# Graph attention block: one 512 KB transposing transfer for both heads of a unit, in place of two of 256 KB

## The chip, the cores and the metric

The kernel runs on one core of a Trainium2 chip. The metric is the device time of one execution in microseconds. Beside it there is one profiled execution, whose span runs from its first to its last instruction.

## The reference, cut to what matters

For each of 16 batches of 1024 rows and 512 columns, the block computes attention with 8 heads of width 64 under a 0/1 matrix, a projection, and two layer norms.

```
qkv = (x @ w_qkv).reshape(b, n, 3, H, hd).transpose(2, 0, 3, 1, 4)
q, k, v = (qkv[0], qkv[1], qkv[2])
attn = jnp.einsum('bhnd,bhmd->bhnm', q, k) * scale
attn = jnp.where(attn_mask[None, None] == 0, -jnp.inf, attn)
attn = jax.nn.softmax(attn, axis=-1)
o = jnp.einsum('bhnm,bhmd->bhnd', attn, v).transpose(0, 2, 1, 3).reshape(b, n, d)
o = o @ w_proj + b_proj
ln = (o - mu) * jax.lax.rsqrt(var + LN_EPS) * ln_gamma + ln_beta
x = _layernorm(x + (o + ln), axis=-1)
```

Products are made from float16 numbers in two parts, a high half (the value rounded to float16) and a low half (what is left of it), so that each product takes three matmuls.

## The kernel before, in words

The work is cut into 64 **groups** (16 batches times 4 pairs of heads) and each group into 8 **units** of 128 query rows. A unit has two **heads**, `ab` 0 and 1, which are numbered on through the group: unit u has heads 2u and 2u+1, so that a group has heads 0 to 15. The program is one loop over groups with the engines' orders written out by hand in 32 slots per group, 4 to a unit; `ORDER` and `ITEMS` spread the other matmuls of a group (projections Q, K, V, the output projection P, transposes O and XT) over the slots.

A head of a unit goes through these steps. TensorE computes scores for both heads (`unit_scores`), VectorE adds the mask and takes the row's minimum into `p32` (L616), ScalarE takes the exponential (`exponential`, L479), then one unit later ScalarE writes the high half `p_hi` (`high_part`, L492) and GpSimd the low half `p_lo` (`low_part`, L722). SyncE sends both halves through a transposing transfer into `pt` (`turn`, L279). TensorE multiplies `pt` by the values three units after the scores (`times_v`, L408 to L410; `PV_LAG` is 3).

The buffers that tie these steps: `p32`, `p_hi` and `p_lo` have `RING` = 4 places, two units. So ScalarE may write the high half of a head only when the transposes of the head four before it have landed (semaphores `turned`, 16 steps for each half). `pt` has `TURNED` = 8 places, four units. SyncE does nothing in the loop but the transposes, in the order high 0, high 1, low 0, low 1 of a unit; each issue is preceded by a wait on `hi_done` or `lo_done` (how many halves ScalarE or GpSimd has finished), and for the high half also on `pv_done`, which tells that the place in `pt` is free.

GpSimd does, between low halves, steps of the layer norm: a power (L735, L738), the bias (L732) and the output (L741). One of the outputs stands between the low halves of heads 12 and 13, the other ahead of head 4. Loads and stores of `x_res` and `x_in` are issued by ScalarE. In every fourth group the next batch's input is transposed on TensorE (XT), in units 3 and 4.

Of the kernel before, what the change touches and what calls it, by code (L numbers as in the profile page):

```python
# [17 lines left out]
UNITS = T  # L18
QUARTERS = 4
SLOTS = UNITS * QUARTERS  # L20
RING = 4
TURNED = 8
# [48 lines left out]
def known(g):  # L71
    return isinstance(g, int)


def active(g, kind):

    if not known(g):
        return True
    low, high = {"A": (0, GROUPS), "Q1": (0, GROUPS), "V0": (0, GROUPS), "V1": (0, GROUPS), "O0": (0, GROUPS),
                 "O1": (1, GROUPS + 1), "Q0": (-1, GROUPS - 1), "K0": (-1, GROUPS - 1), "K1": (-1, GROUPS - 1),  # L80
                 "P0": (PAIRS, GROUPS + PAIRS), "P1": (PAIRS, GROUPS + PAIRS)}[kind]
    return low <= g < high
# [12 lines left out]
def side_done(g, kind):  # L95

    return side_before(g) + (side_index(g, kind) + 1)
# [18 lines left out]
def unit_before(g, u, back):  # L116
    return (g, u - back) if u >= back else (g - 1, u - back + UNITS)
# [7 lines left out]
def wait(eng, sem, value):  # L125

    if known(value) and value <= 0:
        return
    eng.wait_ge(sem, value)


def wait_alone(eng, sem, value):

    if known(value) and value <= 0:
        return
    eng.wait_ge(sem, value)
    eng.nop(nofuse=True)


def attention_block(nc, x, adj, w_qkv, w_proj, b_proj, gamma, beta, out):  # L140
# [3 lines left out]
    with ExitStack() as ctx:  # L144
        def sb(name, shape, dt):
            return ctx.enter_context(nc.sbuf_tensor(name, shape, dt))

        def sem(name):
            return ctx.enter_context(nc.semaphore(name))

        def sems(name, n):
            return [sem(f"{name}{i}") for i in range(n)]

        HI, LO = 0, 1
# [14 lines left out]
        p_hi = sb("p_hi", [P, RING, N], F16)  # L169
        p_lo = sb("p_lo", [P, RING, N], F16)  # L170
        pt = sb("pt", [P, 2, TURNED, T, P], F16)
# [38 lines left out]
        x_in_loaded, x_res_loaded, stored = sems("x_in_loaded", T // 2), sems("x_res_loaded", 2), sems("stored", 2)  # L210
        s_ready, min_done, exp_done = sem("s_ready"), sem("min_done"), sem("exp_done")
        hi_done, lo_done = sem("hi_done"), sem("lo_done")
        turned = sems("turned", TURNED)
        pv_done, recip_done, o_done = sem("pv_done"), sem("recip_done"), sem("o_done")
        side_ready, side_act, side_dve = sem("side_ready"), sem("side_act"), sem("side_dve")
        xt_ready, xt_act, xt_dve = sem("xt_ready"), sem("xt_act"), sem("xt_dve")
# [6 lines left out]
        def bodies(eng, body):  # L223

            for g in range(FIRST_GROUP, LOOP[0]):
                body(g)
            with eng.Fori(LOOP[0], LOOP[1]) as g:
                body(g)
            for g in range(LOOP[1], LAST_GROUP + 1):
                body(g)  # L230
# [9 lines left out]
        def heads(g, u, ab):  # L240

            return g * (2 * UNITS) + (2 * u + ab)

        def turned_before(g, u, ab):

            return g * (32 * 2 * UNITS // TURNED) + 32 * ((2 * u + ab) // TURNED)

        def normalised(g, u):

            return g * (UNITS // NORM_UNITS) + u // NORM_UNITS  # L250
# [5 lines left out]
        @block.sync  # L256
        def _(sp):
            for t in range(T // 2):
                sp.dma_start(x_in[:, t, :, :], x_pairs[t, :, :, :]).then_inc(x_in_loaded[t], 16)
                sp.dma_start(w_in[:, t, :], w_qkv[t * P:(t + 1) * P, :]).then_inc(w_loaded, 16)  # L260
            for t in range(ADJ_SLOTS):
                sp.dma_start(adj_in[:, t, :], adj[t * P:(t + 1) * P, :]).then_inc(adj_loaded[t], 16)
            for t in range(ADJ_SLOTS, T):
                sp.wait_ge(mask_ready, t - ADJ_SLOTS + 1)
                sp.dma_start(adj_in[:, t % ADJ_SLOTS, :], adj[t * P:(t + 1) * P, :]).then_inc(adj_loaded[t % ADJ_SLOTS], 16)
            for kc in range(KC):
                sp.dma_start(wp_in[:, kc, :], w_proj[kc * P:(kc + 1) * P, :]).then_inc(wp_loaded, 16)
            for dst, src in ((gamma_b, gamma), (beta_b, beta)):
                sp.dma_start(dst[:, :], src.rearrange("(o n) -> o n", o=1).broadcast_to([P, D])).then_inc(const_loaded, 16)
            for row in (0, BIAS_LO):  # L270
                sp.dma_start(x_res[row:row + 1, 0, :], b_proj.rearrange("(o n) -> o n", o=1)).then_inc(const_loaded, 16)
            sp.wait_ge(mask_ready, T)

            def turn(g, u, ab, half, source, done):
                head = 2 * u + ab
                wait_alone(sp, done, heads(g, u, ab) + 1)
                if half == HI:
                    wait_alone(sp, pv_done, heads(g, u, ab) - (TURNED - 1))
                sp.dma_start_transpose(pt[:, half, head % TURNED, :, :], source[:, head % RING, :]  # L279
                                       ).then_inc(turned[head % TURNED], 16)  # L280

            def body(g):
                for u in range(UNITS):
                    ug, uk = unit_before(g, u, 1)
                    running = active(ug, "A")
                    if running:
                        turn(ug, uk, 0, HI, p_hi, hi_done)
                        turn(ug, uk, 1, HI, p_hi, hi_done)
                    if running:
                        turn(ug, uk, 0, LO, p_lo, lo_done)  # L290
                        turn(ug, uk, 1, LO, p_lo, lo_done)

            bodies(sp, body)
            for i in range(2):
                sp.wait_ge(stored[i], 16 * B * T // 2)

        @block.tensor
        def _(pe):
# [92 lines left out]
            def times_v(g, u, ab):  # L391

                ug, uk = unit_before(g, u, PV_LAG)
                if not active(ug, "A"):
                    return
                slot = (2 * uk + ab) % TURNED
                wait_alone(pe, turned[slot], turned_before(ug, uk, ab) + 32)
                if ab == 0:
                    if uk % NORM_UNITS == 0:
                        wait_alone(pe, o_done, normalised(ug, uk))  # L400
                    if uk == 0:
                        wait_alone(pe, side_dve, side_done(g, "V1"))
                at = (uk % NORM_UNITS * 2 + ab) * HD
                o = pv_bank[:, at:at + HD]
                for kt in range(T):
                    hi, lo = pt[:, HI, slot, kt, :], pt[:, LO, slot, kt, :]
                    v_hi, v_lo = v_both[:, kt, ab, 0:HD], v_both[:, kt, ab, HD:2 * HD]
                    nc.tensor.matmul(o, hi, v_hi, start=(kt == 0 and at == 0), stop=False, skip_group_check=True)  # L408
                    nc.tensor.matmul(o, hi, v_lo, start=False, stop=False, skip_group_check=True)  # L409
                    mm = nc.tensor.matmul(o, lo, v_hi, start=False, stop=(kt == T - 1), skip_group_check=True)  # L410
                mm.then_inc(pv_done, 1)

            def body(g):
                for u in range(UNITS):
                    if active(g, "A"):
                        unit_scores(g, u)
                    for j in range(QUARTERS):
                        if j % 2:
                            times_v(g, u, j // 2)
                        for kind, i in ITEMS[u * QUARTERS + j]:  # L420
                            side_matmul(g, kind, i)
# [4 lines left out]
        def _(act):  # L426
# [55 lines left out]
            def high_part(g, u, ab):  # L482

                ug, uk = unit_before(g, u, 1)
                if not active(ug, "A"):
                    return
                head = 2 * uk + ab
                before = unit_before(ug, uk, RING // 2)
                if not known(before[0]) or before[0] >= 0:
                    wait(act, turned[(head - RING) % TURNED], turned_before(before[0], before[1], ab) + 32)  # L490
                act.wait_ge(exp_done, heads(ug, uk, ab) + 1)
                nc.scalar.activation(p_hi[:, head % RING, :], p32[:, head % RING, :], ACT.Copy).then_inc(hi_done, 1)  # L492

# [285 lines left out]
```

## Time and profile before

| what | value |
|---|---|
| time, median of 3 runs | 3394.47 us (3382.21 to 3395.74) |
| the profiled execution, its own time | 3382.03 us |
| its span | 3380.2 us |
| granted TensorE clock, mean | 0.98 |
| busy share: TensorE, VectorE, ScalarE, GpSimd | 91%, 67%, 76%, 80% |
| the transposes' DMA queue, share of 16 engines | 87.0% |
| the other loads' and stores' queue | 10.8% |

A busy share is an average over the span. SyncE, which only issues, has no busy share: its issues stand in the timeline as SPq. The share of a DMA queue is the time that its packets took and can pass 1 when packets of one engine overlap.

### The profile page before, as it was taken

How to read it: one execution, taken by the hardware profiler on the slowest of the kernel's cores; microseconds unless marked ns; L12 is line 12 of the kernel's file. 1: busy time of each engine (PE TensorE's matmuls, PEld its weight loads, DVE VectorE, ACT ScalarE, POOL GpSimd, SP SyncE). 2: the span in 40 equal slices, each digit the busy share in tenths (PEclk: the TensorE clock that was granted, in tenths of full speed). 3: DMA queues.
4: the chain of work that ended last, by engine and by line, in shares of the span. 5: the costliest groups of instructions: out<-in, count | busy, mean ns of one | idle time of the engine just before them, and what ended most of it. 6: DMA issues, size and time to landing. Idle time of an engine off the chain costs nothing.

```text
span 3380.2 us, 122707 instructions
## 1 busy us (share of the span) xinstructions
PE 3084.6 (91%) x42624; PEld 1901.9 (56%) x42624; DVE 2273.7 (67%) x4371; ACT 2572.4 (76%) x3723; POOL 2716.8 (80%) x1543
## 2 busy tenths in 40 slices
PE   6888999999999999999999999999999999999984
PEld 3555555555655556555555655556555555655552
DVE  5556676666767677676676766667676666766664
ACT  6777777777878778778787877878777787877770
POOL 3667888787888878878787987878888787987884
PEclk9999999999999999999999999999999999999997
DMA  8999999999999999999999999999999999999992
GB/s 212 179 172 182 203 190 201 185 199 194 201 203 188 204 191 199 202 188 200 190 203 189 203 204 183 204 185 202 205 193 197 190 202 191 203 204 181 203 189 66
DMA packets 2220429, 649.09 MB, mean 192 GB/s; under 512 B 2168146, under 2 KB 2168146, under 8 KB 2220372
## 3 DMA queue, kind: packets, MB, share of 16 engines
q1 hardware_dynamic: 2166372, 548.15, 87.0%
q10 hardware_dynamic: 54000, 100.16, 10.8%
q8 instruction: 38, 0.62, 0.1%
q14 instruction: 19, 0.16, 0.0%
HBM read 77.60 MB, written 33.55 MB: 33 GB/s over the span
## 4 chain that ended last, share of the span: by engine, by line
POOL 52%; issue 32%; SPq 10%; PE 2%; DMA 1%; DVE 1%; POOLq 1%; ACT 0%; ACTq 0%; DVEq 0%
POOL p_lo L722 43%; SPq L279 10%; POOL x_res L741 3%; POOL x_res L732 2%; POOL norm L738 2%; POOL norm L735 2%; PE proj L369 1%; DMA pt<-p_lo 1%; POOLq L721 0%; PE side L351 0%; DMA x_in<-in_x 0%; PE scores_a L387 0%; DMA pt<-in_adj 0%; PE side L316 0%; DVE proj L659 0%
## 5 line engine op out<-in xcount | busy, mean ns | idle before, releaser
L722 POOL TENSOR_TENSOR p_lo<-p,p_hi 128x1024 f16<-128x1024 f32 x1024 | 2170.9, 2137 | 596.7 <-ACT p_hi L492 595.7
L492 ACT ACTIVATE p_hi<-p 128x1024 f16<-128x1024 f32 x1024 | 1052.5, 1051 | 383.7 <-DMA pt<-p_lo 379.6
L479 ACT ACTIVATE p<-p,row_min 128x1024 f32<-128x1024 f32 x1024 | 1167.0, 1141 | 160.2 <-DVE row_min L616 159.0
L616 DVE CUSTOM_DVE_ANT_0 p<-scores_a,mask_q 128x1024 f32<-128x1024 f32 x512 | 626.4, 1223 | 459.1 <-PE scores_b L387 401.8
L408 PE MATMUL pv_bank<-v_both,pt 128*128 128x64 f16 x8192 | 835.1, 194 | 87.4 <-DMA pt<-p_lo 74.8
L408 PEld LDWEIGHTS pv_bank<-v_both,pt 128*128 128x128 f16 x8192 | 743.6, 99 | 218.2 <-issue 147.4
L410 PE MATMUL pv_bank<-v_both,pt 128*128 128x64 f16 x8192 | 836.0, 194 | 0.0
L409 PE MATMUL pv_bank<-v_both,pt 128*128 128x64 f16 x8192 | 835.8, 194 | 0.0
L409 PEld LDWEIGHTS pv_bank<-v_both,pt 128*128 128x128 f16 x8192 | 733.6, 99 | 73.8 <-issue 4.1
L410 PEld LDWEIGHTS pv_bank<-v_both,pt 128*128 128x128 f16 x8192 | 734.3, 99 | 0.0
L616 DVE CUSTOM_DVE_ANT_0 p<-scores_b,mask_q 128x1024 f32<-128x1024 f32 x512 | 624.2, 1219 | 4.8 <-POOL p_lo L722 1.7
L351 PE MATMUL side<-xt_hi,w_hi 128*128 128x512 f16 x1024 | 397.2, 388 | 39.4 <-DVE xt_lo L582 27.8
L351 PE MATMUL side<-xt_lo,w_hi 128*128 128x512 f16 x1024 | 396.0, 387 | 0.0
L351 PE MATMUL side<-xt_hi,w_lo 128*128 128x512 f16 x1024 | 394.1, 385 | 0.0
L387 PE MATMUL scores_a<-k_hi,q_hi 64*128 64x512 f16 x1024 | 307.9, 381 | 68.0 <-DVE row_min L616 65.6
L340 PE MATMUL side<-w_hi,xt_hi 128*128 (+1 forms) x2048 | 366.1, 219 | 1.2 <-DVE q_lo L605 1.2
L340 PE MATMUL side<-w_lo,xt_hi 128*128 (+1 forms) x2048 | 366.9, 219 | 0.0
L340 PE MATMUL side<-w_hi,xt_lo 128*128 (+1 forms) x2048 | 366.7, 219 | 0.0
L369 PE MATMUL proj<-wp_hi,ot 128*128 128x512 f16 x1024 | 335.4, 391 | 27.5 <-DVE x_res L664 27.5
L387 PE MATMUL scores_b<-k_hi,q_hi 64*128 64x512 f16 x1024 | 309.7, 383 | 0.0
L387 PE MATMUL scores_b<-k_hi,q_lo 64*128 64x512 f16 x1024 | 304.4, 377 | 0.0
L387 PE MATMUL scores_a<-k_hi,q_lo 64*128 64x512 f16 x1024 | 304.4, 377 | 0.0
(68 smaller groups left out, 5071.9 us busy)
## 6 DMA issues: line engine op xcount, KB each, us to landing
x_res<-in_x ACTq DMA_DIRECT2D x128, 256.0 KB, 3.7
out<-x_res ACTq DMA_DIRECT2D x128, 256.0 KB, 3.2
x_in<-in_x ACTq DMA_DIRECT2D x63, 512.0 KB, 4.3
pt<-p_hi SPq DMA_TRANSPOSE x1024, 3.4
pt<-p_lo SPq DMA_TRANSPOSE x1024, 3.5
pt<-in_adj SPq DMA_DIRECT2D x8, 512.0 KB, 9.5
ot<-in_L_gnn_w_qkv SPq DMA_DIRECT2D x4, 768.0 KB, 8.8
x_in<-in_x SPq DMA_DIRECT2D x4, 512.0 KB, 7.4
```

Source lines behind the costliest of these rows:

```text
L279: sp.dma_start_transpose(pt[:, half, head % TURNED, :, :], source[:, head % RING, :]).then_inc(turned[head % TURNED], 16)
L340: mm = nc.tensor.matmul(bank[:, c * P:(c + 1) * P], rows[:, k, t * P:(t + 1) * P], w[:, k, OF_V, pair(g), :], start=(i == 0), stop=(i % 12 ...
L351: mm = nc.tensor.matmul(bank[:, :], w[:, k, what, p, :], xt[:, k, half * CH:(half + 1) * CH], start=(i == 0), stop=(i == LENGTH[kind] - 1))
L369: mm = nc.tensor.matmul(proj[:, :], ot[:, (HI, LO, HI)[part], parity(c), k, t, :], (wp_hi, wp_hi, wp_lo)[part][:, k, :], start=(i == 0), s ...
L387: mm = nc.tensor.matmul(scores[ab][:, keys], left[rows, q], right[rows, keys], start=(n == 0), stop=(n == 2))
L408: nc.tensor.matmul(o, hi, v_hi, start=(kt == 0 and at == 0), stop=False, skip_group_check=True)
L409: nc.tensor.matmul(o, hi, v_lo, start=False, stop=False, skip_group_check=True)
L410: mm = nc.tensor.matmul(o, lo, v_hi, start=False, stop=(kt == T - 1), skip_group_check=True)
L479: nc.scalar.activation(p32[:, slot, :], p32[:, slot, :], ACT.Exp, bias=row_min[:, slot:slot + 1], scale=-1.0, accum_out=row_sum[:, head:he ...
L492: nc.scalar.activation(p_hi[:, head % RING, :], p32[:, head % RING, :], ACT.Copy).then_inc(hi_done, 1)
L616: nc.vector.tensor_tensor_reduce(out=p32[:, slot, :], in0=scores[ab][:, :], in1=mask_q[:, u, :], scale=-SCALE, scalar=3.0e38, op0=ALU.add, ...
L722: nc.gpsimd.tensor_tensor(p_lo[:, slot, :], p32[:, slot, :], p_hi[:, slot, :], ALU.subtract).then_inc(lo_done, 1)
```

## The change: what it does

SyncE issues one transposing transfer for both heads' high halves of a unit and one for both heads' low halves, each of 128x2048 elements (512 KB) in place of two of 128x1024. Each waits until both heads' halves are done. There is one `turned` semaphore for each of the four pairs of places in `pt`, in place of one for each place. TensorE waits for it once, ahead of head 0 of the unit, and ScalarE waits for the pair's transposes at each of the two heads.

```diff
-        turned = sems("turned", TURNED)
+        turned = sems("turned", TURNED // 2)
...
-        def turned_before(g, u, ab):
+        def turned_before(g, u):
 
-            return g * (32 * 2 * UNITS // TURNED) + 32 * ((2 * u + ab) // TURNED)
+            return g * (32 * 2 * UNITS // TURNED) + 32 * (2 * u // TURNED)
...
-            def turn(g, u, ab, half, source, done):
-                head = 2 * u + ab
-                wait_alone(sp, done, heads(g, u, ab) + 1)
+            def turn(g, u, half, source, done):
+
+                head = 2 * u
+                wait_alone(sp, done, heads(g, u, 2))
                 if half == HI:
-                    wait_alone(sp, pv_done, heads(g, u, ab) - (TURNED - 1))
-                sp.dma_start_transpose(pt[:, half, head % TURNED, :, :], source[:, head % RING, :]
-                                       ).then_inc(turned[head % TURNED], 16)
+                    wait_alone(sp, pv_done, heads(g, u, 2) - TURNED)
+                sp.dma_start_transpose(pt[:, half, head % TURNED:head % TURNED + 2, :, :].rearrange("p a t n -> p (a t) n"),
+                                       source[:, head % RING:head % RING + 2, :].rearrange("p a n -> p (a n)")
+                                       ).then_inc(turned[u % (TURNED // 2)], 16)
...
-                        turn(ug, uk, 0, HI, p_hi, hi_done)
-                        turn(ug, uk, 1, HI, p_hi, hi_done)
-                    if running:
-                        turn(ug, uk, 0, LO, p_lo, lo_done)
-                        turn(ug, uk, 1, LO, p_lo, lo_done)
+                        turn(ug, uk, HI, p_hi, hi_done)
+                        turn(ug, uk, LO, p_lo, lo_done)
...
-                wait_alone(pe, turned[slot], turned_before(ug, uk, ab) + 32)
                 if ab == 0:
+                    wait_alone(pe, turned[slot // 2], turned_before(ug, uk) + 32)
...
-                    wait(act, turned[(head - RING) % TURNED], turned_before(before[0], before[1], ab) + 32)
+                    wait(act, turned[(head - RING) % TURNED // 2], turned_before(before[0], before[1]) + 32)
```

On SyncE, at the start of the first group, the order before has two issues of each half, each with its wait.

```order
L279 DMA_TRANSPOSE pt<-p_hi 128x8x128 [waits mask_ready,hi_done]
L279 DMA_TRANSPOSE pt<-p_hi 128x8x128 [waits hi_done]
L279 DMA_TRANSPOSE pt<-p_lo 128x8x128 [waits lo_done] x2
L279 DMA_TRANSPOSE pt<-p_hi 128x8x128 [waits hi_done] x2
L279 DMA_TRANSPOSE pt<-p_lo 128x8x128 [waits lo_done] x2
```

At the same place the changed program has one issue of each half.

```order
L280 DMA_TRANSPOSE pt<-p_hi 128x16x128 [waits mask_ready,hi_done]
L280 DMA_TRANSPOSE pt<-p_lo 128x16x128 [waits lo_done]
L280 DMA_TRANSPOSE pt<-p_hi 128x16x128 [waits hi_done]
L280 DMA_TRANSPOSE pt<-p_lo 128x16x128 [waits lo_done]
L280 DMA_TRANSPOSE pt<-p_hi 128x16x128 [waits hi_done]
```

The number of issues is halved and each is twice as large; nothing else moved on this queue. On ScalarE, in the second unit and the units behind it of an early group, the high halves before wait each for a semaphore of its own (here `turned7`, `turned0`, `turned1`).

```order
L492 ACTIVATE p_hi<-p 128x1024 [waits exp_done,turned7]
L479 ACTIVATE p,row_sum<-p,row_min 128x1024 [waits min_done]
L468 ACTIVATE v_both<-side 128x8x64 [waits side_ready,pv_done]
L468 ACTIVATE v_both<-side 128x8x64 [waits side_ready]
L479 ACTIVATE p,row_sum<-p,row_min 128x1024 [waits min_done]
L492 ACTIVATE p_hi<-p 128x1024 [waits exp_done,turned0]
L492 ACTIVATE p_hi<-p 128x1024 [waits exp_done,turned1]
L465 ACTIVATE ot<-side 128x512 [waits side_ready]
```

In the changed program, at the corresponding place, both high halves of a unit wait for one semaphore (`turned3`, then `turned0`).

```order
L490 ACTIVATE p_hi<-p 128x1024 [waits exp_done,turned3] x2
L504 DMA x_res<-in_x 128x512 [waits bias_ready]
L477 ACTIVATE p,row_sum<-p,row_min 128x1024 [waits min_done]
L466 ACTIVATE v_both<-side 128x8x64 [waits side_ready,pv_done]
L466 ACTIVATE v_both<-side 128x8x64 [waits side_ready]
L477 ACTIVATE p,row_sum<-p,row_min 128x1024 [waits min_done]
L490 ACTIVATE p_hi<-p 128x1024 [waits exp_done,turned0] x2
L463 ACTIVATE ot<-side 128x512 [waits side_ready]
```

No instruction changed its place on ScalarE; the first of the two now waits for what only the second waited for.

## Rows read from the trace of the kernel before

**Rows 1.** The page: span, busy time of each engine, DMA queues.
```profile
span 3380.2 us, 122707 instructions
PE 3084.6 (91%) x42624; PEld 1901.9 (56%) x42624; DVE 2273.7 (67%) x4371; ACT 2572.4 (76%) x3723; POOL 2716.8 (80%) x1543
q1 hardware_dynamic: 2166372, 548.15, 87.0%
q10 hardware_dynamic: 54000, 100.16, 10.8%
```
**Rows 2.** Windows over four groups that follow each other; the second holds XT.
```profile
1564.92:1614.46 49.54, 46.39 (x660) 28.37 (x658) 34.01 (x66) 39.05 (x57) 42.38 (x25) 1.00 1.01 201
1614.46:1673.82 59.36, 53.51 (x705) 33.59 (x703) 39.01 (x74) 43.34 (x65) 44.35 (x26) 0.94 0.91 178
1673.82:1719.77 45.95, 44.93 (x652) 28.14 (x649) 33.85 (x68) 38.90 (x57) 40.65 (x24) 1.00 1.03 204
1719.77:1768.42 48.65, 46.40 (x660) 28.36 (x658) 33.92 (x68) 38.99 (x57) 42.61 (x25) 1.00 1.02 206
```
**Rows 3.** Waits of SyncE's queue over the span: total, times, longest.
```profile
SPq L137 <- ACT p_hi L492: 98.1, 31, 15.8
SPq L137 <- POOL p_lo L722: 27.5, 29, 1.4
```
**Rows 4.** Timeline of SyncE in one group: start, us, issues.
```profile
1594.88 2.68 SPq L279 DMA_TRANSPOSE pt<-p_hi  x2
1597.66 2.67 SPq L279 DMA_TRANSPOSE pt<-p_lo  x2
1600.54 2.68 SPq L279 DMA_TRANSPOSE pt<-p_hi  x2
1603.30 3.15 SPq L279 DMA_TRANSPOSE pt<-p_lo  x2
...
1609.43 2.68 SPq L279 DMA_TRANSPOSE pt<-p_lo  x2
1612.33 2.69 SPq L279 DMA_TRANSPOSE pt<-p_hi  x2
1615.11 4.20 SPq L279 DMA_TRANSPOSE pt<-p_lo  x2
```
**Rows 5.** The transposes by tile: ns of an issue, least, median and most.
```profile
L279 SPq DMA_TRANSPOSE pt<-p_hi x1024: 1231/1232/2552, 47.9 to 3295.9; - x171
L279 SPq DMA_TRANSPOSE pt<-p_lo x1024: 1231/1290/3468, 50.7 to 3301.5; - x171
```
**Rows 6.** Low halves by tile: from issue to landing.
```profile
DMA to landing us min/median/max: 3.1/3.5/6.6
```
**Rows 7.** Windows over the first transfer, alone, and over a stretch with transfers queued.
```profile
47.93:49.13 1.20, 1.20 (x25) 1.20 (x23) 1.20 (x3) 1.20 (x2) 1.10 (x1) 1.00 0.00 0
49.20:50.45 1.25, 0.56 (x10) 0.38 (x7) 1.18 (x3) 1.25 (x4) 1.25 (x2) 1.00 1.03 196
1544.35:1545.35 1.00, 1.00 (x10) 0.31 (x5) 0.21 (x2) 0.23 (x1) 0.61 (x1) 1.00 1.27 255
```
**Rows 8.** Timeline of ScalarE: high halves of heads 12 and 13, next group's 0, a load.
```profile
1607.56 2.04 ACT L492 ACTIVATE p_hi<-p 128x1024 f16<-128x1024 f32 x2 [1.82 <-DMA pt<-p_lo]
1620.48 2.00 ACT L492 ACTIVATE p_hi<-p 128x1024 f16<-128x1024 f32 x2 [0.41 <-DMA pt<-p_lo]
1628.04 0.35 ACTq L506 DMA_DIRECT2D x_res<-in_x  x1
```
**Rows 9.** Timeline of GpSimd around the low halves of heads 12 and 13.
```profile
1608.69 2.13 POOL L722 TENSOR_TENSOR p_lo<-p,p_hi 128x1024 f16<-128x1024 f32 x1 [2.33 <-ACT p_hi L492]
1610.78 0.56 POOL L738 TENSOR_TENSOR norm<-mv,minus_half 128x1 f32<-128x1 f32 x1
1611.51 2.08 POOL L741 TENSOR_SCALAR x_res<-x_res,mv,norm 128x512 f32<-128x512 f32 x1 [0.18 <-POOL norm L738]
1613.56 2.14 POOL L722 TENSOR_TENSOR p_lo<-p,p_hi 128x1024 f16<-128x1024 f32 x1
```
**Rows 10.** Waits over the span, other engines.
```profile
ACT p_hi L492 <- DMA pt<-p_lo: 379.6, 496, 3.1
PE pv_bank L408 <- DMA pt<-p_lo: 74.8, 92, 2.7
```

More of the change, by code:

```diff
@@ L284, in body @@
                     ug, uk = unit_before(g, u, 1)
-                    running = active(ug, "A")
-                    if running:
-                        turn(ug, uk, 0, HI, p_hi, hi_done)
-                        turn(ug, uk, 1, HI, p_hi, hi_done)
-                    if running:
-                        turn(ug, uk, 0, LO, p_lo, lo_done)
-                        turn(ug, uk, 1, LO, p_lo, lo_done)
+                    if active(ug, "A"):
+                        turn(ug, uk, HI, p_hi, hi_done)
+                        turn(ug, uk, LO, p_lo, lo_done)
             bodies(sp, body)
```

## The prediction

> **What bounds the kernel now.** I read the page first, for the busy shares and the queues. TensorE is busy 91% of the span, and the packets of the two hardware queues took 97.8% of the DMA engines' time [rows 1]. Either could be the bound, so I looked at whole groups. Outside the XT group a group takes 45.95 to 49.54 us, with TensorE idle for 1.0 to 3.2 us of it; the XT group takes 59.36 with 5.9 idle [rows 2]. TensorE thus could give back at most about 12 us of the 203.5 that four groups take.
>
> Next, SyncE's queue. In the whole span it waited 27.5 us for GpSimd and 98.1 for ScalarE, in 60 waits out of 2048 issues [rows 3]. Its timeline shows the rest of the time filled with issues. From one pair of high halves to the next, 1594.88 to 1600.54, a unit takes 5.66 us: 2.68 for the high halves, 0.10 between, 2.67 for the low halves, 0.21 between [rows 4]. Eight such units are 45.3 us. A group of 49 has a few longer ones, as the low halves at 1615.11 that took 4.20 because other traffic was in the way [rows 4]. So SyncE's issue stream paces most groups. That the data lies ready is seen at heads 12 and 13: the low half of 12 is ready at 1608.69+2.13 = 1610.82 [rows 9] and is issued at 1615.11 [rows 4], 4.3 us later; that of 13 is ready at 1615.70, and SyncE reaches it some 1.4 us behind 1615.11, at about 1616.5.
>
> Last, who waits for the landings: ScalarE's high halves 379.6 us in 496 waits and TensorE's products 74.8 us in 92 [rows 10]. ScalarE's wait is the ring of four heads closing. It costs nothing today, since what it delays still reaches SyncE early.
>
> **What the change removes on SyncE.** A high issue is 1.231 at least and a low one 1.290 in the median [rows 5]. The two high issues of a unit take 2.68, so the gap between them (two waits) is 2.68 - 2.46 = 0.21; the two low ones take 2.67, gap 0.09 [rows 4]. Both gaps go: 0.30 us per unit, 2.4 per group.
>
> **What a 512 KB issue costs** the trace doesn't show. Bounds: twice the small one, 2.46, if the issue is all per piece; and 2.46 - 0.35 = 2.11, if each transposing issue holds a fixed part as large as a plain load's whole issue, 0.35 [rows 8]. The first transfer, which had the queue to itself, tells which is nearer: it was issued at 47.93, nothing moved for 1.2 us, and then its 256 KB flowed for some 1.25 us at 196 GB/s [rows 7]. That is as long as the issue takes, while with transfers queued the engines carry 255 GB/s [rows 7]. So the flow goes at the pace of the issue, and the issue is nearly all per piece. I take 2.46, and 2.11 for the range.
>
> A rule speaks for more. The Trainium skill, "DMA: Bandwidth & Descriptors", section "Anatomy of one DMA", gives a DMA issued from GpSimd a fixed 2.0 us plus its bytes by 436 GB/s; by it two transfers of 256 KB are 5.2 us and one of 512 KB is 3.2, an estimate, and the change would take SyncE and the DMA engines out of the bound altogether. The trace disagrees for these transfers: a landing is 3.1 us or more behind its issue [rows 6], yet the next issue follows after 1.34 [rows 4], so what is fixed already lies beside the next transfer.
>
> **What it adds: latency in the ring.** A pair lands when its last byte does. From issue to landing one head takes at least 3.1 [rows 6]; a pair takes 3.1 + 1.23 = 4.3 at least and 3.5 + 1.23 = 4.7 with the median; I take 4.5. The chain around the ring of two units then is: landing, high 0 (1.05), low 0 and low 1 (2.13 + 2.14), some 0.2 of hand-overs, pair's transfer 4.5: 10.0 us for two units. SyncE's own pace after the change is 5.66 - 0.30 = 5.36 per unit, 10.7 for two. The slack is 0.7 us, where before it was several. Anything that GpSimd puts between eats it.
>
> It puts two things there per group. Heads 12 and 13: the pair of heads 8 and 9, issued from 1603.30 on, would land at about 1608.2 (4.5 after its issue, and 0.4 for the disturbance that its row of 3.15 against 2.67 shows [rows 4]). Then high 12 until 1609.2, high 13 until 1610.2 (each 1.02 by [rows 8]), low 12 from 1609.3 to 1611.5, power and output, which take 1613.56 - 1610.82 = 2.74 [rows 9], low 13 until 1616.4. SyncE stood at 1615.11 even at the old pace, so it waits 1.3; at the new pace it arrives earlier by 0.30 for each of the two or three units since the ring last held it, so the stall is 1.9 to 2.2. The other output stands ahead of both low halves of head 4, where part of it falls into GpSimd's idle time (a pair needs 4.27 of 5.36, leaving 1.1); with the 0.7 of slack it leaves a stall of 2.74 - 1.1 - 0.7 = 0.9 at most, and I take 0.5 to 0.9. Sum: 2.4 to 3.1 us per group. SyncE waited 0.4 per group for GpSimd already (27.5 by 64 [rows 3]), so 2.0 to 2.7 is new, against the 2.4 gained. Net: -0.4 to +0.3 per group, say 0.
>
> **TensorE** now waits for the pair ahead of head 0. Its work is the same. Where SyncE paces, TensorE only shifts by about 1 us against SyncE, once. Where TensorE paces (the XT group's end and the group behind it, idle 1.02 [rows 2]), landings are far ahead, and nothing is gained or lost. At the start of XT, which stands behind the products of a unit, the shift shows. The pair's landing is 1.1 behind that of head 0 now (4.5 against 3.4 after the same issue), less the 0.3 that SyncE gains in a unit: 0.8 us in each of 15 batches, 12 us. Filling and draining the pipeline adds about 1 us each.
>
> **Sum:** 64 x 0 + 12 + 2 = +14, less what the noise of these small terms allows: SyncE's low issues held 0.06 each over the least [rows 5], and if that goes, 0.12 per unit is won, of which at most a third passes the ring, 0.04 x 512 = 20. So 3382 + 14 - 20 = 3376 in the profiled execution's terms. The median of the runs lies 0.37% above it (3394.5 against 3382.0), so 3388.
>
> **Rivals.**
>
> 1. *Faster: the ring doesn't bind.* If the output step finds more room than I count (the loads that disturb SyncE at 1615.11 may fall into the stall), SyncE's gain passes. Per group 2.4, but not more than TensorE's idle time [rows 2]: four groups give 2.4 + 2.4 + 1.0 + 2.3 = 8.1, sixteen times 130 us, 3265. Half of it is likelier: 3325. For it: 379.6 us of waits at ScalarE that cost nothing today. Against: the chain of 10.0 with 2.74 in it. Chance 0.27.
> 2. *Faster still: a fixed issue cost is saved.* With 2.11 an issue, SyncE needs 4.7 per unit; ring and TensorE bound. About 3290. Against: the flow's 1.25 us [rows 7]. Chance 0.05.
> 3. *Slower: the ring of two units binds.* Latency is paid in each group: the stall at heads 12 and 13 over 2.4 us and a second one at head 4 of the full 2.74 less 1.1, so 3.8 and more against 2.4: +1.4 x 48 groups = 67; with TensorE then idle at each late pair, and a refill of 1 to 2 us behind each XT, +90 in all: 3480; half of it 3435. It decides from the point where stalls pass 2.4 us per group. For it: slack of 0.7. A contention as at 1615.11 now holds both heads. Chance 0.28.
> 4. *No change beyond 0.5%*, as in the sum. Chance 0.40.
>
> **Numbers.** 0.5% is 17 us, about what a measurement of this kernel can tell. Faster 0.32, same 0.40, slower 0.28. The range leaves out rival 2 and the far halves of rivals 1 and 3: 3320 to 3455. The forecast's own range is 3372 to 3406.
>
> **What would show it.** Issue: DMA_TRANSPOSE 1024 in all, about 2.46 us each; 2.1 would speak for rival 2, over 2.7 for a cost that grows. Ring: SyncE's waits for GpSimd rise from 27.5 us to 130 or more, mostly ahead of the low pair of heads 12 and 13; if they stay under 60, rival 1 holds. Groups of 49 stay within 48.5 to 50; the one behind XT stays near 46. ScalarE's waits for landings shift to the first high half of a unit. The prediction is wrong if the large transfer flows at another rate than the small one, or if something I hold to be slack (exponentials, mask passes) comes last behind the later landing.

## The result: 3310.99 us, 2.4% faster, and the profile after

| | before | after |
|---|---|---|
| median | 3388.34 us (4 runs) | 3310.99 us (3300.29 to 3315.45, 4 runs) |
| ratio, 95% interval | | 0.9762 [0.9740, 0.9785] |
| span of the profiled execution | 3380.2 us | 3313.6 us |

The forecast was 3388 with a range from 3320 to 3455. The time lies below the range, on the side of the first rival. The page of the changed kernel, the lines that answer to [rows 1]:

```profile
span 3313.6 us, 118885 instructions
PE 3073.8 (93%) x42624; PEld 1908.9 (58%) x42624; DVE 2275.2 (69%) x4371; ACT 2547.9 (77%) x3723; POOL 2717.3 (82%) x1543
q1 hardware_dynamic: 2133604, 548.02, 88.8%
q10 hardware_dynamic: 54000, 100.16, 9.7%
```

The same bytes (in 32768 packets fewer, 32 for each of the 1024 transfers that fell away) and nearly the same busy times stand in a shorter span. Four columns of a window are worth reading: its length, then TensorE's busy time, and at the end the DMA share and GB/s. The windows over the four groups of the changed kernel that answer to [rows 2] (an ordinary group, the XT group, the one behind it, another ordinary one; columns as there):

```profile
1526.35:1573.62 47.27, 46.01 (x666) 28.68 (x665) 33.98 (x67) 38.63 (x57) 42.50 (x25) 1.00 1.06 211
1573.62:1633.20 59.58, 54.18 (x701) 34.24 (x697) 39.12 (x76) 43.26 (x65) 43.24 (x26) 0.91 0.84 167
1633.20:1679.95 46.75, 45.22 (x653) 28.16 (x649) 33.93 (x68) 38.48 (x57) 41.05 (x24) 1.00 1.07 213
1679.95:1727.17 47.22, 45.77 (x659) 28.59 (x658) 33.99 (x68) 38.45 (x57) 42.31 (x25) 1.00 1.06 211
```

The gain is in the two ordinary groups, 49.54 to 47.27 and 48.65 to 47.22; the XT group gives back 0.2 and the one behind it 0.8. Now the waits of SyncE's queue in the changed kernel, which answer to [rows 3]:

```profile
SPq L137 <- POOL p_lo L720: 315.9, 238, 3.2
SPq L137 <- ACT p_hi L490: 174.0, 40, 18.0
```

The stall that the prediction feared is there, and larger than it said: 27.5 us became 315.9, 4.9 per group. Its waits for ScalarE rose as well, from 98.1 to 174.0. SyncE's timeline in the ordinary group, at heads 8 to 13, answers to [rows 4]:

```profile
1561.02 2.95 SPq L280 DMA_TRANSPOSE pt<-p_lo  x1
1564.19 1.97 SPq L280 DMA_TRANSPOSE pt<-p_hi  x1
1566.25 2.59 SPq L280 DMA_TRANSPOSE pt<-p_lo  x1
1569.05 1.92 SPq L280 DMA_TRANSPOSE pt<-p_hi  x1
1574.28 2.88 SPq L280 DMA_TRANSPOSE pt<-p_lo  x1
```

ScalarE's high halves of heads 12 and 13, from the timeline of the same kernel, answer to [rows 8]:

```profile
1566.06 2.01 ACT L490 ACTIVATE p_hi<-p 128x1024 f16<-128x1024 f32 x2 [1.13 <-DMA pt<-p_lo]
```

And GpSimd's steps around their low halves answer to [rows 9]:

```profile
1567.20 2.14 POOL L720 TENSOR_TENSOR p_lo<-p,p_hi 128x1024 f16<-128x1024 f32 x1 [1.43 <-ACT p_hi L490]
1569.29 0.56 POOL L736 TENSOR_TENSOR norm<-mv,minus_half 128x1 f32<-128x1 f32 x1
1570.02 2.08 POOL L739 TENSOR_SCALAR x_res<-x_res,mv,norm 128x512 f32<-128x512 f32 x1 [0.18 <-POOL norm L736]
1572.07 2.14 POOL L720 TENSOR_TENSOR p_lo<-p,p_hi 128x1024 f16<-128x1024 f32 x1
```

Read across: the low pair of heads 8 and 9, issued at 1561.02, lands at 1566.04, and ScalarE starts at 1566.06. The low half of head 13 is ready at 1574.21. SyncE had finished its high issue at 1570.97 and stands idle until 1574.28, 3.3 us. The chain from landing to ready is 8.2 us, as forecast (1608.2 to 1616.4). The landing itself came 5.0 us after its issue (median of the low pairs 4.9), where 4.5 was taken. So the ring was worked out rightly but for that half microsecond, and it costs more than forecast; the kernel still got faster, so a larger fault must be on the other side of the sum. The tile rows of the changed kernel, which answer to [rows 5], point there. A 512 KB issue was to take 2.46 us at least:

```profile
L280 SPq DMA_TRANSPOSE pt<-p_hi x512: 1653/2254/5485, 50.6 to 3226.6; - x171
L280 SPq DMA_TRANSPOSE pt<-p_lo x512: 1440/2440/4102, 54.0 to 3231.1; - x171
```

Its least is 1.44. Its mean, summed over the trace, is 2.47; how the two go together is what the experiments have to tell.

### The profile page after: what moved, and what is told of

Read it like the earlier page. It is cut to its first block, busy times and chain, and to the rows that moved or that the text cites. A ratio compares the mean times of both kernels' runs of the same rounds, so it can differ in the third digit from the quotient of the medians.

```text
span 3313.6 us, 118885 instructions
## 1 busy us (share of the span) xinstructions
PE 3073.8 (93%) x42624; PEld 1908.9 (58%) x42624; DVE 2275.2 (69%) x4371; ACT 2547.9 (77%) x3723; POOL 2717.3 (82%) x1543
## 4 chain that ended last, share of the span: by engine, by line
POOL 52%; issue 32%; PE 5%; SPq 4%; DMA 3%; DVE 1%; ACT 1%; POOLq 1%; ACTq 0%; DVEq 0%
POOL p_lo L720 45%; SPq L280 4%; DMA pt<-p_lo 3%; POOL x_res L730 2%; POOL norm L733 2%; POOL norm L736 2%; POOL x_res L739 1%; PE proj L367 1%; PE side L349 1%; PE scores_a L385 1%; ACT p_hi L490 1%; PE side L338 1%; POOLq L719 0%; PE pv_bank L406 0%; PE pv_bank L408 0%
## 5 line engine op out<-in xcount | busy, mean ns | idle before, releaser
L490 ACT ACTIVATE p_hi<-p 128x1024 f16<-128x1024 f32 x1024 | 1025.8, 1048 | 329.1 <-DMA pt<-p_lo 328.3
L367 PE MATMUL proj<-wp_hi,ot 128*128 128x512 f16 x1024 | 334.9, 390 | 27.5 <-DVE x_res L662 27.5
```

What stands on the lines that cost most here:

```text
L367: mm = nc.tensor.matmul(proj[:, :], ot[:, (HI, LO, HI)[part], parity(c), k, t, :], (wp_hi, wp_hi, wp_lo)[part][:, k, :], start=(i == 0), s ...
```

## The experiments

The theories. SIZE: a large transfer is cheaper than two small ones, in SyncE's issue, in the DMA engines' stream, or both. WAITS: fewer waits on SyncE are the gain. RING: the pair's latency costs the stalls ahead of the low pairs, and takes back part of it. Times are medians. The ratio behind each is to the kernel before, run beside it, which took 3379 to 3389 us; between two experiments the ratios are the better comparison.

**Size by itself (e1).** The changed kernel with a tail behind the last store. It was executed once, and only the tail is read:

```diff
+            for at in range(0, 6, 2):
+                sp.dma_start_transpose(*piece(at, 2)).then_inc(probed, 16)
+                all_landed()
...
+            for at in range(0, 8, 2):
+                sp.dma_start_transpose(*piece(at, 2)).then_inc(probed, 16)
+            all_landed()
```

> The changed kernel with a tail on SyncE after the last store: transposes of 256 KB, 512 KB and 1 MB, first each alone with a wait for its landing, then 8, 4 and 2 of them back to back without waits. Theory ISSUE (a large issue costs SyncE much less than two small ones, and that freed the kernel): alone, issues take 1.23, 1.45 to 1.8 and 2.2 to 2.6 us; back to back the small ones follow each other at 1.28 us and stay there because SyncE paces them, and the large ones move the same 2 MB clearly faster, in under 9 us against 10.3. Theory STREAM (the DMA engines' stream was the bound, with a price per transfer): alone the same short issues, but back to back only the first large issue is short and the following ones grow to 2.4 to 2.6, so that 2 MB take 9.5 to 10 us. My own step on record (all of an issue is per piece) expects 1.23, 2.46, 4.9 alone.

Rows by source line of this kernel: 256 KB alone (L307), 512 KB alone (L310), 1 MB alone (L313), then back to back eight small (L316), four large (L319) and two of 1 MB (L322). Numbers are ns of an issue, and behind each the us from issue to landing:

```profile
L307 SPq DMA_TRANSPOSE pt<-p_hi x3: 1232/1232/1232, 3300.7 to 3306.9; - x3
DMA to landing us min/median/max: 3.0/3.0/3.0
L310 SPq DMA_TRANSPOSE pt<-p_hi x3: 1444/1769/1839, 3310.0 to 3318.6; - x3
DMA to landing us min/median/max: 4.2/4.2/4.2
L313 SPq DMA_TRANSPOSE pt<-p_hi x2: 4797/4824/4850, 3323.0 to 3329.7; - x2
L316 SPq DMA_TRANSPOSE pt<-p_hi x8: 1292/1333/1339, 3336.7 to 3346.3; - x8
DMA to landing us min/median/max: 3.2/3.3/3.4
L319 SPq DMA_TRANSPOSE pt<-p_hi x4: 1761/2374/2912, 3349.6 to 3356.8; - x4
DMA to landing us min/median/max: 4.4/4.8/5.2
L322 SPq DMA_TRANSPOSE pt<-p_hi x2: 4804/4810/4817, 3361.4 to 3366.2; - x2
```

Windows over the three series, 2 MB each, from the first issue to the last landing:

```profile
3336.72:3349.55 12.83, 0.00 (x0) 0.00 (x0) 0.00 (x0) 0.00 (x0) 0.00 (x0) 0.50 0.86 164
3349.59:3361.30 11.71, 0.00 (x0) 0.00 (x0) 0.00 (x0) 0.00 (x0) 0.00 (x0) 0.50 0.96 179
3361.35:3373.00 11.65, 0.00 (x0) 0.00 (x0) 0.00 (x0) 0.00 (x0) 0.00 (x0) 0.50 0.96 180
```

And windows inside one transfer alone: of 512 KB before its data flows, until its issue ends, and behind that; then of 1 MB before its data flows and until its issue ends.

```profile
3310.04:3311.20 1.16, 0.00 (x0) 0.00 (x0) 0.00 (x0) 0.00 (x0) 0.00 (x0) 0.50 0.00 0
3311.20:3311.88 0.68, 0.00 (x0) 0.00 (x0) 0.00 (x0) 0.00 (x0) 0.00 (x0) 0.50 0.99 200
3311.88:3313.80 1.92, 0.00 (x0) 0.00 (x0) 0.00 (x0) 0.00 (x0) 0.00 (x0) 0.50 1.09 202
3322.97:3324.13 1.16, 0.00 (x0) 0.00 (x0) 0.00 (x0) 0.00 (x0) 0.00 (x0) 0.50 0.00 0
3324.13:3327.82 3.69, 0.00 (x0) 0.00 (x0) 0.00 (x0) 0.00 (x0) 0.00 (x0) 0.50 1.14 213
```

Two things. An issue that nothing holds takes 1.23 for 256 KB and 1.44 to 1.84 for 512 KB, not 2.46: at the end of the issue of 1.84, a quarter of the data had flowed and the rest took 1.92 more. And a further small transfer in a row costs the stream (12.83 - 3.2) / 7 = 1.38 us, a further large one (11.71 - 4.4) / 3 = 2.44: two small ones cost 0.31 more than one large. The small issues of the series take 1.33, the large ones 2.4 in the median, each more than alone, so in both series it is the stream that paces. From the first issue to the end of the last, the small series took 10.94 us and the large one 9.55, as theory STREAM had it (9.5 to 10) and not under 9. The step to 1 MB saves nothing more (4.85 against 2 x 2.44). Both readings of SIZE hold in part: per pair an issue that nothing holds falls by 0.6 to 1.0, the stream by 0.3. Where the stream is full, only the 0.3 can show.

**The pair's waits alone (e2).** Two transfers of 256 KB behind one wait for both heads:

```diff
+                wait_alone(sp, done, heads(g, u, 2))
...
+                for head in (2 * u, 2 * u + 1):
+                    sp.dma_start_transpose(pt[:, half, head % TURNED, :, :], source[:, head % RING, :]
+                                           ).then_inc(turned[head % TURNED], 16)
```

> The kernel before with the pair's waits only: SyncE waits for both heads' halves, then issues two transfers of 256 KB back to back, each with its own semaphore; ScalarE and TensorE wait per head as before. Theory ISSUE and theory STREAM: the gain is in the size, so little of it shows here; the two gaps shrink from 0.30 to about 0.1 us per unit, so at most 1.6 us per group, 1% or 3360 us, and 3385 if the stall at heads 12 and 13 takes it back. Rival WAITS (fewer waits on SyncE are the whole gain): 3310.

3350.54 us, ratio 0.9912 [0.9892, 0.9931]. The waits alone give 0.9% of the 2.4%, so WAITS is a part and not the whole; the other 1.5% came with the size (and with the 0.05 us that still lies between the two issues here, and one `turned` for a pair). The gain is larger than expected (3360 to 3385), although the wait for both heads already costs something: SyncE waited 76.9 us for GpSimd, in place of 27.5.

**One half paired (e3, e4).** High and low halves have semaphores of their own; only one of the two goes as a pair:

```diff
+                for ab in ((0,) if paired else (0, 1)):
+                    head, n = 2 * u + ab, 2 if paired else 1
+                    wait_alone(sp, done, heads(g, u, ab + n))
...
+                        turn(ug, uk, HI, p_hi, hi_done, turned_hi, True)
+                        turn(ug, uk, LO, p_lo, lo_done, turned_lo, False)
```

> Only the high halves of a unit go as one 512 KB transfer; the low halves go one by one, with semaphores of their own. ScalarE and TensorE wait for two semaphores. Theory ISSUE: half the saving or more (0.5 to 0.9 us per unit on SyncE), and since TensorE is the next bound nearly the whole gain: 3310 to 3335. Theory STREAM: half the saving of the changed kernel, 3345 to 3355, unless the groups are at TensorE's floor already.

> Only the low halves go as one 512 KB transfer; the high halves go one by one. The ring's latency is as in the changed kernel, and the high half of head 0 is not held back. Theory ISSUE: 3310 to 3335, as with the high halves. Theory STREAM: 3345 to 3355. If the latency of the low pair in the ring costs anything, this one is slower than the kernel with only the high halves paired; by my step on record by 1 to 2 us per group (50 to 100 us).

High halves paired: 3241.19 us, 0.9592 [0.9574, 0.9610]. Low halves paired: 3402.44 us, 1.0072 [1.0051, 1.0093]. Neither alone is half of the change, and both lie outside what was expected of them (3310 to 3355). Pairing the highs gains 4.1%, 139 us. Pairing the lows as well gives 1.7% back, 57 us by the ratios (70 by the bare times, 3241 to 3311). Pairing the lows alone costs 22, although by e1 it should save the stream as much. I had put the second 50 to 100 us above the first, and it is 161. This fits RING: the low pair closes the ring of two units, the high pair, which is issued ahead of the low halves and lands before them, doesn't. SyncE's wait for GpSimd shows it, at 155.8 us with paired lows against 26.5 with paired highs:

```profile
SPq L137 <- POOL p_lo L723: 155.8, 97, 2.2
```

Summed over 30 ordinary groups, the kernel with paired lows takes 1484 us and the kernel before 1486: what the stream saves is taken back, which fits the stalls. Its loss stands in the groups behind XT, 711 against 695 over 15. Both kernels, and e11 below, also split `turned` into a semaphore for the highs and one for the lows. No run changes that alone; with paired lows it brought no gain. Windows of the kernel with paired highs, for four groups in the order used above:

```profile
1499.44:1545.36 45.92, 45.74 (x664) 28.62 (x661) 33.73 (x67) 38.44 (x57) 42.44 (x25) 1.00 1.07 218
1545.36:1602.11 56.75, 52.39 (x697) 33.56 (x694) 38.98 (x76) 43.10 (x65) 42.51 (x25) 0.94 0.86 176
1602.11:1648.03 45.92, 45.71 (x664) 28.59 (x660) 33.73 (x68) 38.44 (x57) 42.44 (x25) 1.00 1.05 214
1648.03:1693.96 45.93, 45.75 (x664) 28.58 (x661) 33.74 (x67) 38.76 (x57) 42.09 (x25) 1.00 1.07 215
```

Three of four groups take 45.9 us with TensorE idle for 0.2: here TensorE is a bound. ScalarE's and TensorE's waits for landings of low halves, in the same kernel, answer to [rows 10]:

```profile
ACT p_hi L493 <- DMA pt<-p_lo: 29.3, 66, 1.9
PE pv_bank L408 <- DMA pt<-p_lo: 18.9, 19, 2.7
```

These two rows can't be set beside the 379.6 and 74.8 us of [rows 10] as they are. With two semaphores the engine makes two waits, and the profile puts a part of them down to "issue". The idle time ahead of ScalarE's high halves holds it all (behind the second bar), here for the kernel before, paired highs and paired lows:

```profile
L492 ACT ACTIVATE p_hi<-p 128x1024 f16<-128x1024 f32 x1024 | 1052.5, 1051 | 383.7 <-DMA pt<-p_lo 379.6
L493 ACT ACTIVATE p_hi<-p 128x1024 f16<-128x1024 f32 x1024 | 1033.5, 1046 | 84.3 <-issue 42.3 <-DMA pt<-p_lo 29.3 <-DMA pt<-p_hi 9.8
L493 ACT ACTIVATE p_hi<-p 128x1024 f16<-128x1024 f32 x1024 | 1026.0, 1048 | 449.7 <-issue 423.3 <-DMA pt<-p_lo 24.9
```

So 383.7 us became 84.3 with paired highs and 449.7 with paired lows. The kernel with paired highs beats both the one before and the changed one.

**Is it SyncE's time (e7, e8)?** Each wait on a finished half is made three times, which adds 0.10 us to the gap ahead of each issue:

```diff
+                for _ in range(3):
                     wait_alone(sp, done, heads(g, u, ab) + 1)
```

> The kernel before, with each wait on hi_done or lo_done made three times, so that SyncE spends some 0.1 us more ahead of each of the 32 issues of a group, and nothing else changes. If SyncE's own time (issue plus waits) paces the kernel before, the whole of it shows, outside the XT units: 2 to 3.2 us per group, 3500 to 3570. If the DMA stream paced it (1.37 us per 256 KB in the probe's row of eight against 1.23 for an issue alone), the issues, which are stretched by the full queue, shrink in its place: under 1 us per group, 3380 to 3430.

> The same tripled waits in the kernel with only the high halves paired, 24 issues per group. Its groups stand at TensorE's floor of 45.9 us, so SyncE should have room: if a large issue is 1.44 us when nothing holds it, SyncE is busy for 8 x (1.44 + 2 x 1.23 + gaps of 0.5) = 35 us of 46, and 2.4 us more per group cost nothing: 3241 to 3250. If the stream or the issues are just below TensorE's floor, it costs 1 us per group or more, 3300.

In the kernel before: 3477.41 us, 1.0294 [1.0262, 1.0327]. In the one with paired highs: 3267.14 us, 0.9673 [0.9641, 0.9704] of the kernel before, 26 us more than without. The tile rows of the first:

```profile
L280 SPq DMA_TRANSPOSE pt<-p_hi x1024: 1231/1231/2573, 49.1 to 3395.4; - x171
L280 SPq DMA_TRANSPOSE pt<-p_lo x1024: 1231/1256/3885, 52.1 to 3399.9; - x171
```

3.2 us per group were added, and the time rose by 98 us, 1.5 per group over all. Summed over the trace, the issues gave way by 84 us, from 2768 to 2684. The highs, most of which stood at their least of 1.23, gave 10 of it; the lows gave 75, and fell from 1.290 to 1.256 in the median. The expectations named 3500 and more for SyncE as the pace and 3430 and less for the stream; it came out between. So in the kernel before SyncE's own time and the stream lie close together, and neither alone is shown to be the bound: 1.23 + 0.21 = 1.44 per high, over the stream's 1.38, and 1.29 + 0.09 = 1.38 per low, right at it. With paired highs 2.4 us per group were added and 0.4 showed: there is room, but not all that the expectation (3241 to 3250) gave it.

**Is it TensorE (e5, e6, e9)?** All three leave out the product of high half and low values, a third of TensorE's work with the values:

```diff
-                    nc.tensor.matmul(o, hi, v_lo, start=False, stop=False, skip_group_check=True)
```

> The kernel before without the matmuls of high half by low values (L409), a third of the products with the values; this part of the computation is left out. TensorE's work falls by 8192 matmuls, some 0.03 us each, 3.8 us per group. If SyncE and the transposes pace the kernel before, groups outside XT stay at 49 and only the XT group and the one behind it get shorter: 3310 to 3350. If TensorE paced it, all of 240 us shows: 3140.

> The changed kernel without the same matmuls; this part of the computation is left out. If its groups (47.2 to 47.4, TensorE idle 1.2) are paced by the transposes and the ring's stalls at heads 12, 13 and 4, they stay within 1 us of that and the kernel lands at 3200 to 3260. If TensorE paces them, they fall by 3 us or more: 3100 to 3130.

> The kernel with only the high halves paired, without the matmuls of high half by low values; this part of the computation is left out. It shows the floor of its transposes below TensorE's 45.9 us per group. By the probe's spacings (2.51 per large and 1.376 per small transfer) the stream is 8 x (2.51 + 2.75) = 42.1 us per group plus what the loads take, 3 to 4.6: 45 to 46.7, so little is gained: 3190 to 3230. If the stream costs less than these spacings say, TensorE's new floor of 42.2 shows: 3000 to 3050.

| kernel | with all products | without | ratio to before, 95% interval |
|---|---|---|---|
| before | 3379 | 3352.06 | 0.9920 [0.9890, 0.9950] |
| changed | 3311 | 3271.56 | 0.9677 [0.9647, 0.9707] |
| highs paired | 3241 | 3191.14 | 0.9418 [0.9398, 0.9438] |

By the ratios, leaving them out gains 0.8% in the kernel before (3310 to 3350 had been expected), 0.9% in the changed one and 1.7% with paired highs. Window over an ordinary group of the kernel before without those products:

```profile
1558.21:1607.91 49.70, 42.95 (x532) 24.59 (x530) 33.86 (x66) 38.90 (x57) 42.37 (x25) 1.00 1.03 200
```

Of the changed kernel without them:

```profile
1512.69:1559.65 46.96, 43.16 (x532) 24.61 (x530) 34.04 (x66) 38.35 (x57) 42.40 (x25) 1.00 1.07 212
```

Of the kernel with paired highs without them, the group behind XT and an ordinary one:

```profile
1583.34:1627.77 44.43, 42.22 (x530) 24.56 (x529) 33.84 (x67) 38.76 (x57) 41.42 (x25) 1.00 1.07 215
1627.77:1674.27 46.50, 42.80 (x532) 24.64 (x530) 33.95 (x66) 38.88 (x57) 42.44 (x25) 1.00 1.06 214
```

TensorE loses over 3 us of work per group (46.39 to 42.95 busy, by [rows 2]), and the ordinary groups stay where they were: 49.7 before, 47.0 changed. So TensorE paced neither. What was gained stands in the XT groups: summed over 15 of them, 36 us in the kernel before, 38 in the changed one and 38 with paired highs, which gains 20 more behind XT. The time of the changed kernel without them, 3272, is above the 3200 to 3260 that I gave this case, so still more of it is the transposes' and the ring's than I thought. The ordinary group of the third is at 46.5, within the 45 to 46.7 worked out from the series of e1, and even 0.6 longer than with all products; why it grew, no run shows. So with paired highs the transposes' floor in an ordinary group lies at TensorE's or just above it, and TensorE is no bound by itself there.

**The stall (e10).** The changed kernel with GpSimd's output step on 8 of 512 columns; the other columns stay without the last normalisation:

```diff
-                    nc.gpsimd.tensor_scalar(xr, xr, mv2[:, i, 0:1]
+                    nc.gpsimd.tensor_scalar(xr[:, 0:8], xr[:, 0:8], mv2[:, i, 0:1]
```

> The changed kernel, but GpSimd's output step (2.08 us, between the low halves of heads 12 and 13 and ahead of head 4) works on 8 of 512 columns; the normalisation of the other columns is left out. Ring theory: the low pair of heads 12 and 13 is ready some 1.9 us earlier, SyncE's stall ahead of it falls from 2.8 to about 1 and that at head 4 from 1.2 to near 0, and groups fall from 47.3 to TensorE's floor of 46 to 46.5: 3240 to 3270. If the stalls are not what separates the changed kernel from the one with only the high halves paired (3241), it stays at 3300 to 3311.

3249.15 us, 0.9585 [0.9559, 0.9610]. Waits of SyncE's queue in this kernel:

```profile
SPq L137 <- POOL p_lo L720: 158.8, 167, 2.0
```

The wait for GpSimd is halved (315.9 to 158.8), and by its ratio the kernel stands where the one with paired highs only does (0.9585 against 0.9592). The output step among the low halves is thus what the low pairs' latency ran into. No run shortens this step in the other kernels; SyncE waited for GpSimd 27.5 us in all in the kernel before and 26.5 with paired highs, so little can lie there.

**Size against waits, for the highs alone (e11).** As e3, but two transfers behind one pair of waits:

```diff
+                    if half == LO or ab == 0:
+                        wait_alone(sp, done, heads(g, u, ab + (2 if half == HI else 1)))
+                    if half == HI and ab == 0:
+                        wait_alone(sp, pv_done, heads(g, u, 2) - TURNED)
```

> As the kernel with only the high halves paired, but the two high halves stay two transfers of 256 KB, issued back to back after one pair of waits; the low halves go one by one with their own waits, and ScalarE and TensorE wait for a high and a low semaphore per head. It differs from the fastest kernel so far (3241) in the size of the high transfer alone. Size theory: a large transfer costs the stream 2.51 against 2.75, and lets SyncE issue in 1.44 what takes 2.46, so most of the 140 us gain is in the size: here only the gap of 0.21 falls to some 0.05, 1.3 us per group of the three in four that SyncE paces, 60 us: 3320 to 3345. Waits theory (it is the missing waits): within 15 us of 3241.

3318.07 us, 0.9815 [0.9786, 0.9843]. Of the 4.1% that paired highs give, 1.9% (63 us) come with the shorter gap and 2.2% (75 us) with the size, the last 0.05 us between the two issues included. Both are real; which of them is larger the intervals don't tell.

## Why the prediction was wrong

- **"What a 512 KB issue costs" is the step that failed,** and with it the term of the sum for the issues, which stood at 0. It took the least of a small issue, 1.23, doubled it, and held the issue to be all per piece. Summed over the trace, the issues fell from 2768 us for 2048 to 2529 for 1024, by 3.7 us per group.
  - The reading behind it took two times of nearly the same length, the issue's 1.23 and the flow's 1.25, for one and the same. [rows 7] spoke against it: nothing moved for 1.2 us, so the data flowed only when the issue was about over, and could not be paced by it. Alone a large issue takes 1.44 to 1.84 and its flow goes on behind it (e1).
  - The 2.46 itself came close to the mean of a large issue, 2.47, but by luck: in a row large issues stand by the stream's 2.44 (e1), and not by twice a small issue's own cost.
  - The other side was priced too low. The two small issues that one large one replaces took 2 x 1.35 in the mean, and the lows alone 1.45, where the prediction counted 1.29, their median, and 0.06 as held time. A few long issues lift the mean and leave the median. By the means a pair saved 0.23 us of issue, near the stream's 0.31 and far from the 0.6 to 1.0 of issues that nothing holds.
- **The sign that was named came true:** "the large transfer flows at another rate than the small one". In a row it costs the stream 2.44 against 2.75 (e1).
- **SyncE's queue added up.** Per group the issues gave 3.7 us. The short gaps between them gave 2.9, where 2.4 was forecast. The idle stretches over 0.5 us took 5.5 (155.7 us over the trace became 507.9), where 2.0 to 2.7 was forecast. That leaves 1.1 us per group, 72 us; less 5 us that the two ends took more, it is the 67 us by which the span fell.
- **What bounds the kernel.** That TensorE didn't pace the ordinary groups was right (e5: less TensorE work leaves the group at 49.7). That SyncE's own time did was half the truth: the DMA stream stood right beside it (e1, e7).
- **Rival 2** had the right mechanism, a part of the issue that isn't per piece (2.11 in its terms; still less in truth), at a chance of 0.05. **Rival 1** named 3325 and so came nearest in size, by luck: it had the ring not bind, and the ring did.
- **The gaps** were right in kind. In e11 the gap between the two highs fell from 0.21 to 0.05, but the one ahead of the first low grew by 0.06, so 0.8 us per group was to be had; 63 us came, 1.0 per group.
- **The ring, 2.4 to 3.1 us of stalls per group:** right in place and sign, too small. SyncE waited 4.9 per group for GpSimd. In the group shown it stood idle for 3.3 ahead of the low pair of heads 12 and 13, where 1.9 to 2.2 was taken, and for 1.45 ahead of that of heads 4 and 5 (1549.05 to 1550.50), where 0.5 to 0.9 was. The landing took 4.9 in place of 4.5, and SyncE arrives earlier than I let it, by the issue's saving, and so waits longer for the same data. Without GpSimd's output step the kernel gains 1.8% more (e10).
- **Load disturbances,** held constant: the two low issues that took 4.20 us at 1615.11 [rows 4] fell together with some 0.5 MB of loads, which flowed from 1616 to 1619 on the other queue. In the kernel before, SyncE could hardly issue faster than the stream drains, so such a delay could not be made good. A large issue is cheap enough to catch up behind it, and that would make up what gap and stream don't explain; but it is argued and not shown, since no run takes it apart from the rest.
- **TensorE** shifting at the start of XT: the XT group rose from 59.36 to 59.58. Right in sign, too small to tell here. The group behind it, where nothing was to be lost, rose from 45.95 to 46.75.
- **The slower side:** the +90 us of rival 3 have no working beside them, and the rows don't give them.
- The issue that would be "2.1 for rival 2, over 2.7 for a cost that grows" was the right place to look, but a median of 2.25 to 2.44 says little: it is mostly time held by the stream. The least value is nearest to the cost, the sum tells what SyncE's queue pays.

## What to carry to other kernels

In this kernel pairing transfers saved something per transfer and cost latency, and the two fell on different transfers. It paid for those that land ahead of what the ring waits for (the high halves: 4.1% faster) and not for those that close the ring (the low halves: 1.7% worse when paired as well). So ask of each transfer who waits for it last before you join it to another. When an issue and the flow behind it last equally long, that doesn't tell which sets which; issue one size alone and in a row, and read the least and the held time apart. Price what a change removes by its mean over the trace, not by its least or its median.

## What the runs showed of the hardware that was not expected

- A transposing issue on SyncE took 1.23 us for 256 KB, 1.44 to 1.84 for 512 KB and 4.8 for 1 MB, each alone (e1). In the first 1.16 us of the issue no data moved, for 512 KB and for 1 MB alike. When the issue of 1 MB ended, its data had flowed for 3.69 us at 213 GB/s, three quarters of it.
- In a row, 2 MB of transposes took 12.83 us in pieces of 256 KB, 11.71 in 512 KB and 11.65 in 1 MB: 0.31 us less for each two of 256 KB that become one of 512 KB, and next to nothing beyond.
- Alone, a 512 KB transpose landed 4.2 us after the start of its issue, a 256 KB one 3.0 (e1).
